# An attention stage: statistics and transposes in a new order, and the causal mask of the row maxima added by VectorE

## What is computed

```
def mla(xn, ...):                      # 16 heads, B = 16, S = 512
    kk = concat(k, rope(k_rope))       # 16 numbers a head
    qq = concat(q, rope(q_rope))
    scores = einsum('bqhd,bkhd->bhqk', qq, kk) * scale
    causal = tril(ones((S, S), bool))
    scores = where(causal, scores, finfo.min)
    probs = softmax(scores)
    return einsum('bhqk,bkhd->bqhd', probs, v) @ W_o
x = x + mla(rmsnorm(x, w_ln1), ...)
x = x + moe(rmsnorm(x, w_ln2), ...)    # router: top 2 of 7 experts
```

## Time and profile before

| what | value |
|---|---|
| profiled execution, whole | 4053.83 us |
| its span, first to last instruction | 4052.0 us |
| PE busy | 3579.4 us (88%) |
| DVE busy | 2892.4 us (71%) |
| ACT busy | 2521.9 us (62%) |
| POOL busy | 2154.4 us (53%) |
| granted TensorE clock, mean | 0.949 |
| mask products of the row maxima (L857, f_Y), to 1350 us | 640 recorded, 264 ns each |
| row maxima (L632) | 896 recorded, 432.4 us |

### The profile page before, as it was taken

How to read it: one execution, slowest core, us unless ns; L and a number is a source line. 1 busy time by engine, 2 the same in 40 slices (tenths; PEclk the granted TensorE clock), 3 DMA queues, 4 the chain that set the end, 5 groups by cost and what they waited for, 6 DMA issues and landing times.

```text
span 4052.0 us, 70010 instructions
## 1 busy us (share of the span) xinstructions
PE 3579.4 (88%) x22072; PEld 2713.9 (67%) x22072; DVE 2892.4 (71%) x5392; ACT 2521.9 (62%) x6537; POOL 2154.4 (53%) x1083
## 2 busy tenths in 40 slices
PE   4899999999998759998799999998999999999887
PEld 1354445445554447777588888888887888888776
DVE  3455655555554222222799999999999999999997
ACT  2545555455454213332788878788887878888783
POOL 3243344334332200000578787787878778787774
PEclk7899999999999779999899999999999999999998
DMA  4333333333332167665222222121222212222221
GB/s 112 97 93 114 101 117 98 110 106 112 94 111 74 34 182 211 208 210 176 87 73 103 84 81 99 65 99 71 104 84 81 98 66 99 71 104 84 81 80 40
DMA packets 286364, 416.64 MB, mean 103 GB/s; under 512 B 78261, under 2 KB 250678, under 8 KB 263672
## 3 DMA queue, kind: packets, MB, share of 16 engines
q1 hardware_dynamic: 273048, 380.79, 29.6%
q0 software_dynamic: 12288, 33.57, 2.3%
q10 hardware_dynamic: 864, 0.10, 0.1%
HBM read 330.30 MB, written 83.17 MB: 102 GB/s over the span
## 4 chain that ended last, share of the span: by engine, by line
DVE 36%; issue 11%; PE 2%; POOL 1%; DVEq 1%; ACT 1%; DMA 0%; SPq 0%; POOLq 0%; ACTq 0%
DVE m_S L1774 8%; DVE m_PR L1774 8%; DVE m_S L1766 8%; DVE m_PR L1766 8%; DVE m_ub L1751 2%; DVE m_yz L1785 1%; DVE m_x L1735 1%; POOL m_ub L1554 1%; DVEq L1765 1%; DVE m_th_x L1743 1%; ACT m_dA L1663 1%; PE m_F L1884 0%; PE m_Y L1922 0%; PE m_F L1858 0%; PE m_F L1934 0%
## 5 line engine op out<-in xcount | busy, mean ns | idle before, releaser
L1554 POOL TENSOR_TENSOR m_ub<-m_Bb,m_dtx 128x2048 f32<-128x2048 f32 x254 | 1157.0, 4567 | 280.6 <-PE m_Y L1922 176.1
L1663 ACT ACTIVATE m_dA<-m_dt,m_a_neg 128x128 f32<-128x128 f32 x4096 | 1211.1, 388 | 129.6 <-DVE m_S L1774 129.2
L1922 PE MATMUL m_Y<-m_ub,m_ident 128*128 128x128 f32 x8192 | 956.2, 278 | 62.7 <-DVE m_ub L1751 62.4
L1922 PEld LDWEIGHTS m_Y<-m_ub,m_ident 128*128 128x128 f32 x8192 | 939.5, 194 | 73.8 <-DVE m_ub L1751 73.5
L632 DVE TENSOR_REDUCE f_nm<-f_Y 128x1 f32<-128x512 f32 (+3 forms) x896 | 432.4, 531 | 308.9 <-PE f_Y L857 306.8
L552 ACT ACTIVATE f_pt<-f_X 128x512 f32<-128x512 f32 (+1 forms) x704 | 372.5, 556 | 406.8 <-PE f_X L857 403.5
L1766 DVE SCALAR_TENSOR_TENSOR m_PR<-m_dA,m_S 128x512 f32<-128x512 f32 x512 | 355.8, 695 | 26.1 <-POOL m_ub L1554 7.5
L1766 DVE SCALAR_TENSOR_TENSOR m_S<-m_dA,m_PR 128x512 f32<-128x512 f32 x512 | 354.8, 693 | 12.0
L1774 DVE CUSTOM_DVE_ANT_1 m_S<-m_S,m_ub 128x512 f32<-128x512 f32 x512 | 353.2, 690 | 0.8 <-issue 0.8
L1774 DVE CUSTOM_DVE_ANT_1 m_PR<-m_PR,m_ub 128x512 f32<-128x512 f32 x512 | 353.2, 690 | 0.2 <-DVE m_PR L1766 0.2
L1751 DVE TENSOR_TENSOR m_ub<-m_S,m_Cb 128x512 f32<-128x512 f32 x512 | 349.5, 683 | 0.0
(11 more groups left out here) (233 smaller groups left out, 6009.6 us busy)
## 6 DMA issues: line engine op xcount, KB each, us to landing
m_Bb<-m_bc_dram SPq DMA_DIRECT2D x64, 1024.0 KB, 4.7
m_Cb<-m_bc_dram SPq DMA_DIRECT2D x64, 1024.0 KB, 6.3
f_parts_dram<-f_parts SPq DMA_DIRECT2D x32, 768.0 KB, 4.1
f_kst<-f_parts_dram SPq DMA_DIRECT2D x192, 128.0 KB, 2.6
f_qst<-f_parts_dram SPq DMA_DIRECT2D x192, 128.0 KB, 2.6
e_rows<-sorted_rows SPq DMA_DIRECT2D x70, 256.0 KB, 2.8
e_wg<-Wg SPq DMA_DIRECT2D x70, 256.0 KB, 2.9
e_wu<-Wu SPq DMA_DIRECT2D x70, 256.0 KB, 4.0
```

What stands on the lines that cost most here:

```text
L1554: pool.tensor_tensor(ub[:, h, i, :, :], Bb[:, s, :, :], dtx[:, m, None, s * SN:(s + 1) * SN].to_broadcast([P, NST, SN]), ALU.mult).then_in ...
L1663: last = act.activation(dA[:, h, i, n, :], dtt[:, par, m, s * SN:(s + 1) * SN], ACT.Exp, scale=a_neg[:, m, n:n + 1])
L1922: last = pe.matmul(Y[:, i * SN:(i + 1) * SN], ident[:, :], ub[:, h, 1 + i, n, :], start=False, stop=(n == NST - 1), skip_group_check=True)
```

## The change

The mask products of `s1` go: the last score product closes the bank. VectorE's `tensor_reduce` becomes `tensor_tensor_reduce`, which adds a causal row (0, and -1e30 above the diagonal of the last 128 columns), scales by -1, keeps the minimum in its accumulator and writes the sum back over the bank. The two heads of an `s1` item with j = 2, one instruction before, are two now. In the list, the statistics behind `wo` 1 and `wo` 3 become items of their own (`x2s`, slots 28 and 32), which GpSimd's block at `wo` 3 follows; `h2` and `h2a` move back one slot, `nmt` moves up from 56 to 54, and `u` 1 back from 55 to 57, so that `nmt` comes before it; `pfx` moves from 58 to 59.

```diff
-    mask_q = sb("f_mask_q", [P, P], bf16)
+    causal = sb("f_causal", [P, SEQ], bf16)
...
-                          (29, "wo", 2, 0), (30, "mid", 1, 0), (31, "wo", 3, 0), (33, "xrload", 0, 0), (34, "keep", 1, 0), (34, "h2", 0, 0), (35, "h2a", 0, 0),
+                          (28, "x2s", 0, 0), (29, "wo", 2, 0), (30, "mid", 1, 0), (31, "wo", 3, 0), (32, "x2s", 1, 0), (33, "xrload", 0, 0), (34, "keep", 1, 0), (35, "h2", 0, 0), (36, "h2a", 0, 0),
...
-                          (46, "g", 0, 0), (48, "xn", 0, 0), (49, "u", 0, 0), (50, "nm", 0, 0), (52, "rank", 0, 0), (52, "g", 1, 0), (55, "u", 1, 0),
-                          (56, "nmt", 0, 0), (58, "pfx", 0, 0), (59, "bn", 0, 0)):
+                          (46, "g", 0, 0), (48, "xn", 0, 0), (49, "u", 0, 0), (50, "nm", 0, 0), (52, "rank", 0, 0), (52, "g", 1, 0),
+                          (54, "nmt", 0, 0), (57, "u", 1, 0), (59, "pfx", 0, 0), (59, "bn", 0, 0)):
...
-            fixed(pool.memset(mask_q[:, :], 0.0))
-            fixed(pool.affine_select(out=mask_q[:, :], in_=mask_q[:, :], compare_op=ALU.is_ge, fill=MASKED,
+            fixed(pool.memset(causal[:, :], 0.0))
+            fixed(pool.affine_select(out=causal[:, SEQ - P:SEQ], in_=causal[:, SEQ - P:SEQ], compare_op=ALU.is_ge, fill=MASKED,
...
-            if kind == "wo" and i == TT - 1:
+            if kind == "x2s" and i == 1:
 
                 pool.wait_ge(stats2_done, TT * (b + 1))
...
-            def row_max(k, out, cols, last=True):
-                ins = dve.tensor_reduce(out, cols(full(k, r)), AX.X, ALU.max, negate=True)
+            def row_max(k, out, c0, n, last=True):
+                if c0 == 0:
+                    dve.wait_ge(*filled(k, r))
+                    dve.sem_inc(taken)
+                cols = bank_of(k, r)[:, c0:c0 + n]
+                ins = dve.tensor_tensor_reduce(out=cols, in0=cols, in1=causal[:, SEQ - n:SEQ], scale=-1.0, scalar=-MASKED,
+                                               op0=ALU.add, op1=ALU.min, accum_out=out)
...
-                    row_max(("s1", i, j, 0), nm[:, 3, h + j:h + j + 1], lambda bank: bank[:, :])
-                    row_max(("s1", i, j, 1), nm[:, 2, h + j:h + j + 1], lambda bank: bank[:, 0:384], last=False)
-                    row_max(("s1", i, j, 1), nm[:, 0, h + j:h + j + 1], lambda bank: bank[:, 384:512])
+                    row_max(("s1", i, j, 0), nm[:, 3, h + j:h + j + 1], 0, 512)
+                    row_max(("s1", i, j, 1), nm[:, 2, h + j:h + j + 1], 0, 384, last=False)
+                    row_max(("s1", i, j, 1), nm[:, 0, h + j:h + j + 1], 384, 128)
                 else:
-                    row_max(("s1", i, j, 0), nm[:, 1, h:h + 2], lambda bank: bank[:, :].rearrange("p (h n) -> p h n", h=2))
+                    row_max(("s1", i, j, 0), nm[:, 1, h:h + 1], 0, 256, last=False)
+                    row_max(("s1", i, j, 0), nm[:, 1, h + 1:h + 2], 256, 256)
...
                                   xn[:, 2 * n:2 * n + 2, :], ALU.add).then_inc(free_sem(("wo", n), r), 1)
+            if kind == "x2s":
+                n = i
                 for t in range(2 * n, 2 * n + 2):
                     dve.wait_ge(*used(("wo", n), r))
                     dve.bn_stats(st2[:, t, :], x2[:, t, :]).then_inc(stat2, 1)
...
-                    scores(bank, 0, h + j, 3, p)
-                    full(("s1", i, j, 0), r, hide(bank, 384, P, 1, mask_q))
+                    full(("s1", i, j, 0), r, scores(bank, 0, h + j, 3, p))
                     bank = free(("s1", i, j, 1), r)
                     scores(bank, 0, h + j, 2, p)
-                    scores(bank, 384, h + j, 0, p)
-                    full(("s1", i, j, 1), r, hide(bank, 256, P, 2, mask_q))
+                    full(("s1", i, j, 1), r, scores(bank, 384, h + j, 0, p))
...
-                    scores(bank, 256, h + 1, 1, p)
-                    full(("s1", i, j, 0), r, hide(bank, P, 2 * P, 2, mask_q))
+                    full(("s1", i, j, 0), r, scores(bank, 256, h + 1, 1, p))
```

More of the change, by code:

```diff
@@ L147, in build_attn @@
     STAGE.update({kind: 0 for kind in ("mvx", "mvs", "xrload", "xn", "s2", "pv", "oc", "so", "sl", "rp", "ro", "rl", "ym")})
-    STAGE.update({kind: -1 for kind in ("sl1", "rp1", "ro1", "rl1", "ym1", "wo", "h2", "h2a", "ht", "route", "lg", "rank", "pfx", "g", "u", "d")})
+    STAGE.update({kind: -1 for kind in ("sl1", "rp1", "ro1", "rl1", "ym1", "wo", "x2s", "h2", "h2a", "ht", "route", "lg", "rank", "pfx", "g", "u", "d")})
     STAGE.update({"scat": -2, "d": -2, "xload": 3, "bn": 3})
@@ L665, in do @@
                     dve.wait_ge(nm_step, 5 * b)
+                if isinstance(b, int) and b == 0:
+                    dve.wait_ge(const_ready, N_CONST)
                 if j < 2:
-                    row_max(("s1", i, j, 0), nm[:, 3, h + j:h + j + 1], lambda bank: bank[:, :])
-                    row_max(("s1", i, j, 1), nm[:, 2, h + j:h + j + 1], lambda bank: bank[:, 0:384], last=False)
-                    row_max(("s1", i, j, 1), nm[:, 0, h + j:h + j + 1], lambda bank: bank[:, 384:512])
-                else:
-                    row_max(("s1", i, j, 0), nm[:, 1, h:h + 2], lambda bank: bank[:, :].rearrange("p (h n) -> p h n", h=2))
+                    row_max(("s1", i, j, 0), nm[:, 3, h + j:h + j + 1], 0, 512)
+                    row_max(("s1", i, j, 1), nm[:, 2, h + j:h + j + 1], 0, 384, last=False)
+                    row_max(("s1", i, j, 1), nm[:, 0, h + j:h + j + 1], 384, 128)
+                else:
+                    row_max(("s1", i, j, 0), nm[:, 1, h:h + 1], 0, 256, last=False)
+                    row_max(("s1", i, j, 0), nm[:, 1, h + 1:h + 2], 256, 256)
             if kind == "mvx":
@@ L839, in scores @@
             n = P * (qb + 1)
-            pe.matmul(bank[:, c0:c0 + n], qst[p][0:KS, h, qb * P:(qb + 1) * P], kst[p][0:KS, h, 0:n],
-                      start=(c0 == 0), stop=False, skip_group_check=True)
+            return pe.matmul(bank[:, c0:c0 + n], qst[p][0:KS, h, qb * P:(qb + 1) * P], kst[p][0:KS, h, 0:n],
+                             start=(c0 == 0), stop=True, skip_group_check=True)
         def scores_t(bank, c0, h, kb, p):
```

## The result

| | before | after |
|---|---|---|
| median | 4059.67 us (9 runs, 4046.68 to 4073.20) | 4079.16 us (9 runs, 4071.02 to 4084.63) |
| profiled execution | 4053.83 us | 4081.45 us |
| span, granted clock | 4052.0 us, 0.949 | 4079.6 us, 0.943 |
| DVE busy in twelve rounds (247 to 1217 us, 243 to 1215 us) | 547 of 970 us | 578 of 972 us |

The ratio after to before is 1.0053 [1.0038, 1.0068]: about 20 us slower, at the edge of what the prediction called no change, with twice its shift (+10 us). The profiled executions lie 27.6 us apart, a little more than the medians. The first gate product of the expert stage behind attention tells how much of that was lost in attention: view of the tile e_G, first before, then after (start of the first and of the last, shape).

What follows compares the result with a forecast made beforehand. The prediction took a latency chain followed by TensorE's own stream to bound each attention round. Its terms gave +1.2 us a round, +10 us in all on 4053.83: 4062 us, called no change (within 0.5%, chance 0.42), range 4000 to 4094.

Steps and rivals of the forecast that it cites:

- The bound: In attention, a latency chain ends each round, not PE's 93% busy share; from `xs` on it is a constant 27 us.
- Where the wait goes: At the bank of `g` 1, the 2.7 us wait moves from `nmt` to `u` 1, 4 to 8 us every round.
- L: Latency chain from `wo` 3 to release of the bank of `g` 1, 30.6 us a round; would grow by 1.57.
- The accumulator: Extra cost of VectorE's new row-maximum instruction, taken at 80 ns each, between 7 and 145 ns.
- Rival D: Slower: the new row-maximum instruction costs 145 ns or more extra; 4076 us, or 4090 at 300 ns; chance 0.15.
- `u` 1 behind the release: `u` 1 would stand behind the bank's release instead of `nmt` and one `s2`; R grows by 1.0 us a round.
- The clock: TensorE's low clock behind the stall, in R, would come every round and sometimes double: +0.9 us a round.
- R: PE's own stream from the bank's release to the next `wo` 3, almost without waits, 49.8 us a round.
- Rival C: Slower: two or three low-clock stretches at `u` 1's stall cost 4.3 us a round, net +3.1; 4093 us; chance 0.19.
- The masks: Dropping `s1` mask products saves 3.6 us a round: 2.26 off R, the other 1.36 hidden by the wait.
- The sum: Over attention: +1.2 us a round in 14 rounds, +17 us; the two rounds before them -7 us; +10 us in all.
- Rival B: Faster: no such chain, `nmt`'s stall goes and PE's saving counts in full; 3938 us, or 3996 for half; chance 0.24.

Runs made afterwards that it cites:

- `keep` first: The kernel before with only the store put ahead of the reload of x in SyncE's queue: 4134.4 us, ratio 0.9901 to before.
- `g` 1 first: The changed kernel with item `g` 1 ahead of the rank chain in slot 52: 4130.8 us, ratio 0.9887 to the kernel before.
- masks alone: The kernel before with only the masks moved to VectorE, in the old list order: 4155.3 us, ratio 0.9952 to before.
- before, again: The kernel before, unchanged, run on another chip to have its trace from there: 4181.1 us (one run).

## Why the prediction was right, and where it was not

- **The bound.** Right. Not the 93% of TensorE but the chain from `wo` 3 over `xs`, SyncE's queue and the rank chain to the bank of `g` 1 ends the round. From `xs` on its length stayed constant after the change (26.4 to 26.8 us), and to shorten it gave 1.0% (`keep` first, in the kernel before) and 1.7% (`g` 1 first, in the kernel after).
- **Where the wait goes.** Right: from `nmt` to `u` 1, in all nine rounds; forecast 4 to 8 us, measured 4.1 on the first chip.
- **L.** Forecast +1.57, measured +0.6 (0.8 in the round shown). The statistics do come 1.2 us later, but the store lands 0.5 us faster, and the accumulator costs next to nothing. This term was too large by 0.9.
- **The accumulator.** Taken at 80 ns between 7 and 145. Its own duration is 142 ns, near the upper bound, but in a row of maxima it adds 0.01 us each. The upper bound was a duration, not a distance of starts; with mask products I had made that distinction, here not. Rival D is out as it was put: VectorE's maxima hold PE up more (26.6 instead of 13.0 us), but inside L.
- **`u` 1 behind the release.** Forecast +1.0, measured +1.1 beside the clock. Right.
- **The clock.** Forecast +0.9 a round, measured +1.2 (estimate, from 1.6 to 2.8 in R). Right in direction and nearly in size. Rival C put 4.3 us for the stretches where 2.8 stand, and decided from 3.0.
- **The masks.** The term that was most wrong in R. Forecast -2.26, counted from distances of starts in one item; measured -1.5 on the first chip, in a piece of the round that is at full clock in most rounds. On the other chips masks alone give -1.2 us a round, and with the new order or with the wait gone nothing. Their price must be taken with the clock they leave behind and with the waits for VectorE that open.
- **The sum.** +0.6 (L) and +0.9 (R) are the measured +1.5 a round, forecast +1.2 from +1.57 and -0.36. The total is near because two errors of opposite sign meet: L too large by 0.9, R too small by 1.2, 0.8 of it the masks. That is luck. So is the total over the stage: the sum had 14 equal rounds, but four rounds behind the ninth grew by 3.0 us each, and the two rounds that no chain binds gained 1.6 us until the first `xs`, not 7.
- **Rival B** is out: no stall was removed. But its number came near for another edit: with the bank's reader moved ahead of the chain the kernel gains 1.1%.

The Trainium skill ("TensorE: Matmul & The Clock Gate", Part 1) holds that the slow clock is the default and activity lifts it. The experiment with products in the wait agrees: 3.57 us for `u` 1 without them, 1.82 with them. The prediction cited it and said that by it the term could double; measured it was 1.2 against the 0.9 that the sum had kept.

## What to carry to other kernels

A busy share of 93% can hide a latency chain: look for a wait of once in a round whose chain has a constant length, and price each edit by whether it lies inside the chain or behind it. Before moving a wait to another fill of a ring, list for every bank who takes it next, and what stands behind the wait on the engine at its half clock. Work taken from TensorE may come back as a lower clock and as longer waits for the engine that took it over, so try the order first and the saving after it.

## What the runs showed that was not expected

- **Fewer products, lower clock.** 0.94 to 0.90 over nine rounds by taking the mask products out, with no stall for the bank in either kernel, and 114 us of TensorE's work at the low clock instead of 77; and unused products in a wait made the kernel faster (4196.1 to 4174.4 us).
- **An instruction whose duration costs nothing.** The accumulator's read, 142 ns in 1024 rows, starts with the next maximum and adds about 10 ns.
- **Another chip, another round.** The kernel before takes 4173 to 4178 us on three chips, and took 4060 in the first result. A round is 10 us longer there, and that stretch is where GpSimd issues its scatters (L534): VectorE has idle time ended by "remote", 62.0 us in 19 times from 312 to 1040 us, of which the first chip has none. Timeline of DVE (before, again):

```profile
632.47 0.76 DVE L632 TENSOR_REDUCE f_nm<-f_Y 128x1 f32<-128x384 f32 x2 [2.17 <-remote]
...
637.12 1.35 DVE L632 TENSOR_REDUCE f_nm<-f_Y 128x1 f32<-128x512 f32 x3 [3.89 <-remote]
```

and of GpSimd in the same stretch:

```profile
625.06 1.06 POOL L534 DMA_INDIRECT sorted_rows<-f_h,f_info  x1 [0.66 <-issue]
...
634.04 0.96 POOL L534 DMA_INDIRECT sorted_rows<-f_h,f_info  x1 [0.31 <-issue]
```

What the cores wait for there is open; no run removed the scatters. The change itself costs +1.5 us a round with this surplus and without.
